# Later chunk of a gated-recurrence and expert kernel: the experts' first factor by a Strassen step on operands the gates already use

## The reference, cut to what matters

```python
xn = _layernorm(x)                       # x: 8 x 2048 tokens x 2048 features
r = sigmoid(xn @ Wa.T + ba);  i = sigmoid(xn @ Wx.T + bx)      # two 2048x2048 gates
a = exp(-8 * softplus(-Lam) * r);  u = sqrt(1 - a**2) * (i * xn)
y = scan over tokens of h = a*h + u
logits = xn @ Wr.T + br;  e = argmax(softmax(logits));  g = max(softmax(logits))
h = einsum('nd,erd->ner', xn, A)         # A: 8 experts x 64 ranks x 2048 = 512 x 2048
out = x + y + g * (h[:, e] @ B[e].T) / 64
```

## Time and profile before

| | before |
|---|---|
| median of 3 runs | 1632.46 us (1632.03 to 1636.09) |
| the profiled execution, time | 1628.9 us |
| its span, slowest core (core 1) | 1627.0 us (cores: 1617.5 to 1627.0) |
| PE busy | 1567.0 us, 96% |
| DVE busy | 1075.6 us, 66% |
| ACT busy | 697.6 us, 43% |
| second chunk's expert stage on PE | about 844.6 to 943.8 us |
| first, second gate stage on PE | about 179 to 844.6, 943.8 to 1604 us |

### The profile page before, as it was taken

One profiled execution on the slowest core, in us unless ns is written; L12 is line 12 of the kernel. 1 busy time (PEld: TensorE's weight loads), 2 busy tenths in 40 slices (PEclk: granted clock), 3 DMA queues, 4 the chain that ended last, 5 costly groups with the idle time before them and its releaser, 6 DMA issues.

```text
span 1627.0 us, 21800 instructions; the slowest of 8 cores (1617.5 to 1627.0 us)
## 1 busy us (share of the span) xinstructions
PE 1567.0 (96%) x7488; PEld 733.5 (45%) x7488; DVE 1075.6 (66%) x1439; ACT 697.6 (43%) x946; POOL 102.5 (6%) x188
## 2 busy tenths in 40 slices
PE   3999999999999999999998999999999999999997
PEld 2554544444444444444443354444444444444443
DVE  5687649686868676756566965838374747465656
ACT  4644453534353525343433436353534343434442
POOL 0100010001010101000000001000000000000000
PEclk9999999999999999999999999999999999999999
DMA  7501264555464556533346224432323233332331
GB/s 243 143 35 53 78 180 145 149 169 175 150 158 157 154 150 170 154 115 126 105 137 178 74 85 125 135 122 90 123 86 110 100 112 108 100 120 94 116 115 52
DMA packets 74220, 202.99 MB, mean 125 GB/s; under 512 B 9728, under 2 KB 10112, under 8 KB 74112
## 3 DMA queue, kind: packets, MB, share of 16 engines
q1 hardware_dynamic: 54288, 136.40, 28.5%
q0 software_dynamic: 18816, 65.02, 11.7%
q10 hardware_dynamic: 1008, 0.18, 0.1%
HBM read 168.01 MB, written 33.55 MB: 124 GB/s over the span
## 4 chain that ended last, share of the span: by engine, by line
PE 75%; DVE 12%; DMA 5%; issue 5%; ACT 2%; SPq 1%; DVEq 0%; ACTq 0%
PE pb L95 75%; DVE ch L95 4%; DVE ring L95 2%; DVE wf L95 2%; DMA aux<-x 2%; DMA wf<-xnd 2%; DVE st L95 1%; DMA xh<-x 1%; ACT ch L95 1%; SPq L93 1%; DVE xl L95 1%; DMA wf<-x 0%; ACT xh L95 0%; DVEq L91 0%; ACT ring L95 0%
## 5 line engine op out<-in xcount | busy, mean ns | idle before, releaser
L95 PE MATMUL pb<-xh,ring 128*128 128x512 f16 x3824 | 1155.5, 379 | 5.9 <-DVE ch L95 3.7
L95 PE MATMUL pb<-xl,ring 128*128 128x512 f16 x1912 | 725.5, 379 | 0.0
L95 PEld LDWEIGHTS pb<-xh,ring 128*128 128x128 bf16 x3824 | 374.8, 98 | 459.0 <-issue 12.4
L95 ACT ACTIVATE ring<-wf 128x1024 bf16<-128x1024 f32 x224 | 232.6, 1049 | 232.0 <-DVE wf L95 122.4
L95 PEld LDWEIGHTS pb<-xl,ring 128*128 128x128 bf16 x1912 | 187.3, 98 | 222.9 <-issue 1.0
L95 DVE TENSOR_TENSOR ring<-wf,ring 128x1024 bf16<-128x1024 f32 x224 | 271.7, 1218 | 20.6 <-ACT ring L95 20.5
L95 DVE TENSOR_TENSOR ch<-ch,pb 128x512 f32<-128x512 f32 x176 | 116.7, 683 | 157.5 <-ACT ch L95 86.7
L95 PE MATMUL pb<-ring,btb 128*128 128x512 bf16 x768 | 175.9, 379 | 0.0
L95 DVE TENSOR_TENSOR wf<-wf 128x1024 f32<-128x1024 f32 (+1 forms) x144 | 166.4, 1160 | 8.5 <-DVE wf L95 5.5
L95 ACT ACTIVATE ch<-pb 128x512 f32<-128x512 f32 x110 | 64.3, 594 | 210.8 <-PE pb L95 210.7
L95 DVE TENSOR_TENSOR btb<-ch,btb 128x512 bf16<-128x512 f32 x34 | 23.5, 692 | 162.3 <-ACT btb L95 162.3
(11 more groups left out here) (104 smaller groups left out, 833.7 us busy)
## 6 DMA issues: line engine op xcount, KB each, us to landing
wf<-wu SPq DMA_DIRECT2D x128, 512.0 KB, 4.8
ring<-hgd POOLq DMA_DIRECT2D x64, 512.0 KB, 4.7
ch<-xT SPq DMA_DIRECT2D x64, 256.0 KB, 7.1
out<-ch POOLq DMA_DIRECT2D x56, 256.0 KB, 4.6
ch<-btu SPq DMA_DIRECT2D x32, 256.0 KB, 2.7
aux<-x SPq DMA_DIRECT2D x32, 256.0 KB, 4.2
aux<-xT SPq DMA_DIRECT2D x32, 256.0 KB, 5.5
xnd<-aux POOLq DMA_DIRECT2D x32, 256.0 KB, 2.7
```

Of the source, the lines that this page charges most:

```text
L95: i = calls[it[1]]()(*it[2], **it[3])
```

## The change

The first chunk stays as it was. In the second, h for 1024 tokens by 512 columns is computed by the same seven-product scheme, on the seven combinations that the gates use. This needs combinations of A's blocks: four of them (`S1` to `S4` in the scheme's terms) are made in the first gate stage (`sums_of_rows`, odd units, two steps of 16-bit split and a store to the new DRAM tensor `es`); the statistics wait while it works, and the first normalization waits until all eight are done. A's own blocks are loaded again as parts of `ad` (`e_load1`, by POOL, pieces of 512 bytes). `x_and_e` replaces `x_and_h`: P1 and P2 (`e_first`, 6 matmuls for each of 16 steps, 4 groups of router matmuls), then all of `x_second1(0)` and `x_second1(1)`, the copy of P1 out (`e_first_out`), and P6, P7, P5, P3 for each kt (`e_step`, 24 matmuls), then 6 groups of router matmuls (`e_logits`). P4, which needs combination 3, is two items E0 and E1 of 24 matmuls, items 4 and 5 of the second gate stage (146 items), whose weights SP loads in pieces of 256 bytes. Combination 3 is made by `x_third1` after everything else of the stage: kt 0 to 2 after `prep(1)` and ahead of `combine(2)`, 3 to 7 in the background of items 0 to 2, ahead of the gates there. B12 is no longer kept. `x_second1` makes 4 ACT and 8 DVE instructions, `x_third1` 1 and 3.

```diff
+    T2B = (13, 2, 1, 18, 10, 3, 4, 5)
+    t2_ok = {}
     def x_second1(kt):
         (b1, B12, l1), (b2, B22, l2) = x2_ld[kt]
-        f1, f2 = combos(kt, B12, l1, B22, l2)
-        xb_give(b1, f1)
-        xb_give(b2, f2)
+        c22 = cast(B22, l2, 6, kt)
+        b3, T1 = xb_next()
+        q = DVE.op("tensor_tensor", T1, B12, xc(0, kt), ALU.subtract,
+                   after=[l1, xb_free[b3], x_ok[0][kt]])
+        q = DVE.op("tensor_tensor", T1, T1, xc(0, kt, True), ALU.subtract, after=[q])
+        cT1 = cast(T1, q, 5, kt)
+        b4, T3 = xb_next()
+        q3 = DVE.op("tensor_tensor", T3, B22, B12, ALU.subtract,
+                    after=[l1, l2, xb_free[b4]])
+        cT3 = cast(T3, q3, 2, kt)
+        T2 = ch[T2B[kt]][:]
+        q2 = DVE.op("tensor_tensor", T2, B22, T1, ALU.subtract,
+                    after=[l2, q, ch_free[T2B[kt]]])
+        cT2 = cast(T2, q2, 1, kt)
+        xb_give(b1, [q, q3])
+        xb_give(b2, residue(B22, c22, 6, kt) + [q2, q3])
+        xb_give(b3, residue(T1, cT1, 5, kt) + [q2])
+        xb_give(b4, residue(T3, cT3, 2, kt))
+        t2_ok[kt] = residue(T2, cT2, 1, kt)
+    def x_third1(kt):
+        v = ch[T2B[kt]][:]
+        q = DVE.op("tensor_tensor", v, xc(4, kt), v, ALU.subtract,
+                   after=[t2_ok[kt], x_ok[4][kt]])
+        q = DVE.op("tensor_tensor", v, v, xc(4, kt, True), ALU.add, after=[q])
+        c = cast(v, q, 3, kt)
+        pay()
+        def end():
+            ch_free[T2B[kt]] = residue(v, c, 3, kt)
+        owed.append(end)
...
+    SROW = ((8, 9), (10, 11), (12, 13), (14, 15), (4, 5), (6, 7), (0, 1), (2, 3))
+    EU, EC, ED, EF = (4, 5), (6, 7), (1, 3), (2, 0)
...
+    def e_load1(kt):
+        for r in range(2):
+            e_ok["t1", kt] = POOL.dma(
+                AR[kt][:, 512 * r:512 * r + 512].rearrange("p (w n) -> p w n", w=2),
+                ad[2 * kt + r].rearrange("p (w n) -> p w n", w=2)[:, :, 0:256],
+                s_ar[kt], after=[ad_ok[2 * kt + r], ar_free[kt]])
+    def e_load2(kt):
+        for w, a in enumerate(SROW[kt]):
+            e_ok["t2", kt, w] = POOL.dma(AR[a], es[kt, w], s_ar[a],
+                                         after=[es_ok[kt, w], ar_free[a]])
...
+    def e_first(n):
+        kt = KORD[n]
+        k, second = kt % 8, kt >= 8
+        o = 512 if second else 0
+        for i in range(2):
+            b = (EC if second else EU)[i]
+            hi = AR[k][:, o + 128 * i:o + 128 * i + 128]
+            lo = AR[k][:, o + 256 + 128 * i:o + 256 + 128 * i + 128]
+            p = e_mm(b, hi, lo, 4 if second else 0, k, k == 0, second and k == 7,
+                     [e_ok["t1", k], bank_free[b] if k == 0 else None],
+                     k == 7 or (second and i == 1))
+            e_ok["P2" if second else "P1", i] = p
+        if second:
+            ar_free[k] = [p]
+        if n % 4 == 3:
+            r = x_rows(0, 0, (k - 1, k)) + x_rows(4, 8, (k - 1, k))
+            e_ok["lg"] = router(r, EF[0], n == 3, n == 15)
...
+    def e_first_out(lgb, blocks):
+        for i in range(2):
+            b = blocks[i]
+            t = ACT.op("activation", ch[b][:], bank[EU[i]][:], AF.Copy,
+                       after=[e_ok["P1", i], ch_free[b]])
+            bank_free[EU[i]] = [t]
+            t = DVE.op("tensor_tensor", ch[b][:], ch[b][:], bank[EC[i]][:], ALU.add,
+                       after=[t, e_ok["P2", i]])
+            bank_free[EC[i]] = [t]
+            hok1[0][i] = t
...
+    def e_step(kt):
+        for name, bs, w, o, j in (("P6", EU, 0, 0, 1), ("P7", ED, 0, 256, 2),
+                                  ("P5", EC, 1, 256, 5), ("P3", EF, 1, 0, 6)):
+            a = AR[SROW[kt][w]]
+            for i in range(2):
+                hi = a[:, o + 128 * i:o + 128 * i + 128]
+                lo = a[:, 512 + o + 128 * i:512 + o + 128 * i + 128]
+                p = e_mm(bs[i], hi, lo, j, kt, kt == 0 and name != "P6", kt == 7,
+                         [e_ok["t2", kt, w], bank_free[bs[i]] if kt == 0 else None],
+                         kt == 7 or (name == "P3" and i == 1))
+                e_ok[name, i] = p
...
+    def e_out(t1b, t2b):
+        u = []
+        for i in range(2):
+            u.append(ACT.op("activation", ch[t2b[i]][:], bank[EU[i]][:], AF.Copy,
+                            after=[e_ok["P6", i], ch_free[t2b[i]]]))
+        for i in range(2):
+            x = t1b[2 + i]
+            t = DVE.op("tensor_tensor", ch[x][:], ch[t2b[i]][:], bank[ED[i]][:],
+                       ALU.add, after=[u[i], e_ok["P7", i], ch_free[x]])
+            e_ok["U3", i] = t
+        for i in range(2):
+            y = t2b[2 + i]
+            hok1[1][2 + i] = DVE.op("tensor_tensor", ch[y][:], ch[t1b[2 + i]][:],
+                                    bank[EC[i]][:], ALU.add,
+                                    after=[e_ok["U3", i], e_ok["P5", i], ch_free[y]])
+        for i in range(2):
+            v = ch[t2b[i]][:]
+            t = DVE.op("tensor_tensor", v, v, bank[EC[i]][:], ALU.add,
+                       after=[u[i], e_ok["U3", i], e_ok["P5", i]])
+            e_ok["C12", i] = t
+        for i in (1, 0):
+            v = ch[t2b[i]][:]
+            hok1[1][i] = DVE.op("tensor_tensor", v, v, bank[EF[i]][:], ALU.add,
+                                after=[e_ok["C12", i], e_ok["P3", i]])
+    def e_logits(lgb):
+        g = [x_rows(0, 0, range(0, 4)), x_rows(0, 0, range(4, 8)),
+             x_rows(5, 0, range(0, 4)), x_rows(5, 0, range(4, 8)),
+             x_rows(6, 8, range(0, 4)), x_rows(6, 8, range(4, 8))]
+        for n, rows in enumerate(g):
+            r = router(rows, EU[0], n == 0, n == 5)
...
+    ITEMS1 = ITEMS[:4] + [(0, "E0"), (0, "E1")] + ITEMS[4:]
...
+            if name[0] == "E":
+                i = int(name[1])
+                for w in range(2):
+                    hg_ld[name] = SP.dma(
+                        ring[s][:, 1024 * w:1024 * w + 1024].rearrange(
+                            "p (k n) -> p k n", k=8),
+                        ad.rearrange("(k r) p n -> r p k n", r=2)[
+                            1, :, :, 512 * w + 256 + 128 * i:
+                            512 * w + 384 + 128 * i],
+                        s_e4[i],
+                        after=[ring_free[s]] + [ad_ok[n] for n in range(16)])
+                return
...
+    def x_and_e(gp):
+        for b in (BCB):
+            ch_free[b] = ch_free[b] + bc["last"]
+        for n in range(16):
+            if n + 11 < 16:
+                x1_ld[n + 11] = xn_load(0, KORD[n + 11])
+            if n + 7 < 16:
+                x_first1(n + 7)
+            if n + 6 < 16:
+                x_first1_lo(n + 6)
+            if n in (5, 7):
+                x_second1_load((n - 5) // 2)
+            e_first(n)
+        for r in range(4, 8):
+            e_load2(r)
+        lgs = []
+        for r in range(8):
+            x_second1(r)
+            if r + 2 < 8:
+                x_second1_load(r + 2)
+            if r == 1:
+                lgs.append((e_first_out(LT[0], HT[0]), LT[0]))
+                e_step(0)
+            if r > 1:
+                e_step(r - 1)
+            if r == 7:
+                for s, a in ((2, 10), (3, 12), (4, 14), (0, 0)):
+                    ring_free[s] = list(ar_free[a])
+                wf_free[4], wf_free[5] = list(ar_free[4]), list(ar_free[6])
+                btb_free[:] = ar_free[8]
+                begin()
+                for w in range(4):
+                    wf_free[w] = xb_free[2 * w] + xb_free[2 * w + 1]
+                load(0, "A21", None)
+                load(0, "A22", None)
+        prep(0)
+        e_step(7)
+        ring_free[1] = list(ar_free[2])
+        e_out(HT[0], HT[1])
+        lgs.append((e_logits(LT[1]), LT[1]))
+        prep(1)
+        for r in range(3):
+            x_third1(r)
+        combine(2)
+        return lgs, hok1
...
+        kt = ew["kt"]
+        r0, r1 = aux[0], aux[1]
+        lo_, hi_ = slice(0, 256), slice(256, 512)
+        if ew["stage"] == 1 and t >= ew["at"] + 2:
+            a = DVE.op("tensor_tensor", r1[:, hi_], r0[:, hi_], r1[:, hi_], ALU.add,
+                       after=ew["ld"])
+            b = DVE.op("tensor_tensor", r0[:, hi_], r0[:, lo_], r0[:, hi_],
+                       ALU.subtract, after=[a])
+            q = DVE.op("tensor_tensor", r0[:, lo_], r1[:, hi_], r0[:, lo_],
+                       ALU.subtract, after=[a, b])
+            d = DVE.op("tensor_tensor", r1[:, lo_], r1[:, lo_], r0[:, lo_],
+                       ALU.subtract, after=[q])
+            ew["h"] = [ACT.op("activation", half(ch[BCB[w]][:].bitcast(BF16), 0),
+                              aux[w][:], AF.Copy, after=[b, q, d, ch_free[BCB[w]]])
+                       for w in range(2)]
+            ew["stage"] = 2
+        elif ew["stage"] == 2:
+            for w in range(2):
+                sg = ch[BCB[w]][:].bitcast(BF16)
+                h = ew["h"][w]
+                p = DVE.op("tensor_tensor", half(sg, 1), aux[w][:], half(sg, 0),
```

(29 more changed lines are left out.)

171 lines of the change are left out of this document (107 added, 64 removed).

## The result

The changed kernel takes 1705.53 us (median; 1685.68 to 1886.23 in 4 runs), the kernel before 1632.24 us (1630.28 to 1636.09, 4 runs). The ratio is 1.036, 95% interval 1.029 to 1.042; it leaves out two executions of the changed kernel in which cores ran at a mean clock of 0.84 to 0.95, and the other two (1685.68 and 1696.49) are 59 us above the kernel before. The forecast was 1639.5. The profiled execution took 1696.49 us, its span is 1695.0.

What follows compares the result with a forecast made beforehand. PE was taken as the bound, busy 1567.0 of 1627.0 us. Terms 0.8 - 18.5 + 10.4 + 13.0 + 2.5 - 1.0 = +7.2 on 1628.9 gave 1636.1, plus 3.6 predicted as 1639.5; own range 1634 to 1645, overall 1629 to 1649.

Steps and rivals of the forecast that it cites:

- the first of the sum: First gate stage: the sums' added DVE work, taken as 24 us in units 1 and 3, lengthens the stage by only 0.8 us.
- its cover: First gate stage: H weight loads are asked for 15 us or more ahead, covering a DVE lag of a few us.
- Expert stage: Second chunk's expert stage: fewer matmuls despite new waits, 80.6 us against 99.1, -18.5 (-25.1 to -14.3).
- The hole before P6: Expert stage, before e_step: PE waits for P1's bank copy in ACT's queue, 6 us plus 2.5 for the clock.
- G: The start of the second gate stage, from which its forecast times are counted.
- Second gate stage: E0 and E1 +10.4, late router's chain with gate_rows at G+36.7 +13.0, clock +2.5, a wait gone -1.0.
- The rest of the sum: All terms but the first gate stage's: 7.2 - 0.8 = +6.4 us.
- The last addition of the forecast: From the profiled execution's 1636.1 to the median of runs: 3.6 us added, given as 1639.5.
- C: Rival, first gate stage: added DVE work holds PE about 1 us in a dozen even-unit items, +10, 1649; chance 0.09.
- B: Rival, second gate stage: router's chain not late, gate_rows hole under 3 us, 1627.2, faster; chance 0.13.
- A: Rival, expert stage: loads land early, hole before e_step 1.9 us without clock loss, 1632.9, no change; chance 0.20.
- D: Rival, expert stage: POOL's loads starve while DVE works, e_first starts some 12 us late, 1651; chance 0.06.

Runs made afterwards that it cites:

- E0: Not a run, no run e0 exists: one of two items of 24 matmuls that make P4 in the changed kernel's second gate stage; no time of its own measured.
- e1: Kernel before plus only the sums of the weights' rows in the first gate stage, read by nothing: 1646.4 us, +21.6.
- e4: Changed kernel with the sums' ACT casts issued one slot later, behind the DVE operations they read: 1642.7 us, 15 us under the changed kernel.
- e3: Changed kernel with the sums' time slots kept but empty, so statistics and norms stay late: 1646.7 us, 9.5 above e2.
- e2: Changed kernel without the sums, second weights read from A's rows in DRAM: 1637.1 us, +12.4 over the kernel before.
- e11: e10 with x_third1(2) back ahead of unit 0: 1640.7 us, +11.4 over the kernel before, ratio 1.0074; unit 1's gate not the reference's.
- e12: e11 without the sums (the edit of e2): 1628.2 us, -1.1 against the kernel before, ratio 0.9991.
- e10: e9 with P1's bank copy right behind x_second1(0): cores 4 to 7 at 1650.0 us against 1643.7 before; low-clock chip, no verdict.
- e9: Changed kernel, sums last, two x_third1 blocks ahead of the gates, E0 and E1 items 6 and 7: cores 4 to 7 1657.6 us, before 1643.7; no verdict.
- e13: e11 with E0 and E1 as items 5 and 6, everything computed: 1634.9 us, +12.1 over the kernel before, ratio 1.011.
- e8: Kernel before with 16 small ACT operations that PE waits for in unit 4, one hole: 1631.7 us, +7.0, ratio 1.0039.
- e5: Changed kernel with the router's chain two items later, E0 and E1 as items 5 and 6, combine(2) ahead of x_third1(0): 1653.7 us, ratio 1.037.
- e7: e5 and e6 together, with the copy of P1's banks right behind x_second1(0): 1643.1 us, ratio 1.017.
- e6: Changed kernel with the sums after the last norm, norms at their old place, casts as in e4: 1645.8 us, +21.1, ratio 1.014.

## Why the prediction was wrong

**The step that failed** is the first of the sum: "More DVE work near there can add up to 6 us, and moved statistics can take 2 away; I take +0.8. ACT and PE get nothing here that shows", with its cover, "That covers a DVE lag of a few us". Measured are +21.5 on core 7 and +21.6 with the sums alone (e1). The volume of DVE's work was right (23.9 us for 24). The mistake was to weigh the volume and not the places in the other queues, and one place on DVE itself: "They lie in units 1 and 3" holds for the operations of six of the eight sums, and the busy share of 34 of 46.6 us that I gave to that place came from a window that lay across two units. Three things take the term's place:
- The casts stand at the head of ACT's queue before DVE has done what they read, with a bank's copy behind them (5.51 us idle, PE 4.68), worst for the two sums in even units. With the casts one slot later 15 us came back (e4).
- The statistics and the norms come later. I followed them to item 139 and priced that at nothing; it costs 9.5 us (e3 against e2). One part is the stores of norms ahead of H loads in POOL's queue: PE waits 3.06 us on core 7, 9.12 on core 4. The loads' slow landing (9.9 us on core 7, 15.4 on core 4) is in these waits, too.
- A store of a sum waits 14.57 us for DVE, and an H load behind it is late. The load starts about 9 us late and lands in 8.4, and with that the "15 us or more" of cover are used up.

These prices overlap (15 + 9.5 is more than 21.6), so that a split of the 21.6 us into three is not to be had from these runs. Nor is it shown why the sums cost 12.5 us at their last place, with the casts moved and the norms early; on core 2 PE's waits of 0.5 us and more up to the stage's end are 16.6 us in e11 and 4.3 in e12. That difference is as large as the price, and 13.9 of the 16.6 are for DVE; which of DVE's operations make them late is open.

**Expert stage,** -18.5 forecast, -14.5 on core 7 and -14.3 in e2: at the end of its bounds (-25.1 to -14.3). `e_first` took 30.7 instead of 27.4, in part since step 1 waited 4.12 us for its residue, where 0.83 plus 1.3 to 2.1 was forecast. The hole before P6 was 6.67 (forecast 6); in e2, 7.63. From P6's first product to G are 46.8 us: `e_step` without holes takes 44.0, that is 41.4 and 2.6 for the clock (forecast 2.5), and the logits take 2.8. e10 shows the hole's cause as given, the copy's place in ACT's queue.

**Second gate stage,** +24.9 forecast, +23.7 and +25.0 measured. Gates at G+24.3 and `gate_rows` at G+36.7 came out to the tenth, the hole is 12.43 where 13 was said. The clock cost less than the 2.5 us forecast, about 1.2: it fell to 0.50 at 971.9, 2.4 us into the hole, and was back at 1.00 at 985.6, 3.7 us behind its end. The chain worked out operation by operation in queue order held; the stage where I had counted only busy time did not. e9 confirms the cause: with two of the eight blocks ahead of `gates` instead of seven, and four behind the first spread, `gate_rows` begins 9.1 us earlier.

**The rest of the sum** (+6.4) measured +12.4 in e2: 4.2 of the difference in the expert stage, 1.5 ahead of it. The last addition of the forecast, 1636.1 + 3.6, gives 1639.7 and not 1639.5, which changes nothing.

**The rivals.** C named the place, with too small a price and another mechanism: it expected a dozen waits for DVE of 1 us and was held unlikely because the work stands in odd units. The large waits are for ACT, in even units, and for H weights, in odd ones. B is out by G+36.7, A by the hole. D: POOL's issues beside a busy DVE took 0.54 to 0.56 us each in the mean, as before, and 0.70 to 0.72 those for `hgd` and for the new weight loads in pieces of 512 bytes. No issue stands still; the long idles of POOL are waits of its own queue. The rule of the Trainium skill (SBUF — State Buffer, "SBUF: two separate sides") did not come into play at the issues of this case: the trace shows none that is starved. Some H loads landed slowly, as said above, and for that no run shows a cause.

**The whole time.** The undisturbed cores lose 33 to 36 us, the executions that the ratio compares 59. A run's time is that of its slowest core, and in the profiled execution the pairs 0, 1 and 4, 5 lost a further 20 us or so to the clock. Nothing in the prediction had that.

## What to carry to other kernels

Background work on an engine with spare time must be priced in every queue that it enters: for each instruction, what it waits for when it reaches the head, and what stands behind it (bank copies on ACT, weight loads on POOL). Work that pushes a planned task later moves that task's stores too, in front of new neighbours. Where a wait ends a chain on DVE, look which of the operations ahead of it could stand behind it, before giving the chain more time.

## What the runs showed of the hardware

Pairs of cores (0 and 1, 2 and 3, ...) ran for about 160 us (158.8 to 162.5) at a granted clock of 0.81, between TensorE's two levels of 1.2 and 2.4 GHz, with PE busy throughout and the other cores of the die at 1.00. The windows of the changed kernel, cores 4 and 7 (columns: stretch, its length, busy time and count of PE, PEld, DVE, ACT and POOL, granted clock, DMA share, GB/s):

```profile
371.00:376.00 5.00, 4.87 (x12) 1.75 (x13) 5.00 (x7) 1.88 (x2) 2.56 (x5) 0.50 0.25 69
...
400.00:500.00 100.00, 99.82 (x388) 42.74 (x389) 63.97 (x90) 35.05 (x47) 4.87 (x9) 0.81 0.52 135
...
550.00:640.00 90.00, 87.53 (x405) 39.50 (x405) 60.99 (x76) 34.24 (x45) 9.72 (x18) 1.00 0.70 155
```

```profile
400.00:500.00 100.00, 97.09 (x457) 44.75 (x456) 71.94 (x100) 44.50 (x58) 7.56 (x14) 1.00 0.59 173
```

388 matmuls in 100 us against 457: that is the clock, not a wait. The Trainium skill (TensorE: Matmul & The Clock Gate, "Part 1: The HAM clock gate (the "warmup" mystery)") tells of a limiter that takes a die to 13/16 of the clock once three of its cores run dense matmuls. The size agrees (13/16 is 0.8125). The rest does not: here it took two cores of a die, for a part of the span, while all eight worked alike. Other forms occur: in a few executions a whole die had a mean clock of 0.81 to 0.82 (cores 4 to 7 in one of e13, 1904 to 1924 us), and on the chip of e1 to e4 cores 4 to 7 had stretches of 15 us at 0.81 about every 80 us.

After a hole of 5.71 us at 369.09 in e8's profiled run, core 6 was at 1.00 again from 372 to about 540 us, and at 0.81 only then. Windows of core 6:

```profile
372.00:400.00 28.00, 28.00 (x131) 12.67 (x130) 11.66 (x15) 12.18 (x19) 2.18 (x4) 1.00 0.32 102
400.00:520.00 120.00, 119.61 (x555) 54.12 (x554) 87.77 (x110) 49.41 (x63) 13.06 (x24) 1.00 0.66 169
...
560.00:690.00 130.00, 130.00 (x497) 53.87 (x496) 75.41 (x94) 51.80 (x68) 12.43 (x23) 0.81 0.53 139
```

Core 7 came to 0.81 with it, but it had one more hole just ahead, with a clock of 0.50 (its timeline and window):

```profile
533.77 3.75 PE L95 MATMUL pb<-ch,onesf 128*128 128x128 f32 x16 [5.20 <-DVE ch L95]
...
531.00:537.00 6.00, 3.23 (x15) 3.26 (x16) 5.04 (x13) 3.24 (x5) 0.00 (x0) 0.50 0.15 57
```

So this 0.81 began 170 us behind the hole that was put in, and 8 us behind the end of another. In the profiled executions of the changed kernel, of e5 and e13 a hole of 2.6 to 6.6 us stands 5 to 11 us ahead of the pair's 0.81 as well, in e7 none does, and cores 2, 3, 6 and 7 of the changed kernel had the same holes without it.

Counted are pairs with a mean clock below 0.98 where the die's other pair is above it. They came in 4 of 16 cases with the changed kernel, in 5 of 16 with e5, in 2 of 42 with e8 and in none of 50 with the kernel before on the chip of e5 and e8. That looks like an effect of PE's holes. But e6, on that chip too, had none in 16, and on the chip of e13 the kernel before had them in 7 of 58, beside 8 of 42 with e13. So holes may make them likelier; that they cause them is not shown, and what does is open.
